# Layer 0 of a four-layer graph network in another order: P first, bias rows and polynomial between the first products

## The chip, the cores and the metric

The kernel runs on one core of a Trainium2 chip. Five queues work side by side on it: TensorE (PE, matmuls and transposes), VectorE (DVE), ScalarE (ACT), GpSimd (POOL) and SyncE (SP, which issues the DMAs). Each takes its own instructions strictly in the order in which the program wrote them, and waits for semaphores. The metric is the device time of one launch in microseconds (us). Three runs of the kernel before took 1326.53, 1332.32 and 1336.32 us.

## The reference, cut to what matters

Four layers run one after another on `x` (16 batches of 512 nodes by 128 features) with one adjacency matrix `adj` (512 x 512). Only layer 0, `x = x + L0(relu(layernorm(x)))`, is touched:

```python
h = jnp.einsum('bnd,ed->bne', x, fc_in_w) + fc_in_b
alph = sigmoid(alpha_train)[:, None]
w_eff = w * clip(d, 0, 1) @ w.T
dt = 1 / 8
def euler_step(h, _):                       # 8 times
    ax = jnp.einsum('nm,bmd->bnd', adj_mx, h)
    f = alph * 0.5 * (ax - h) + h @ w_eff - h + x0
    return (h + dt * f, None)
```

The eight steps are linear in `h`, so the kernel computes them as a polynomial of degree 8 in two matrices: P (512 x 512, `dt/2 * alph * (adj - I)`) from the left and R (128 x 128, `(1 - dt) I + dt * w_eff`) from the right. The input bias gives a polynomial too, in P applied to a vector of ones and R applied to the bias row.

## The kernel before, in words

`build_front` does layer 0, and beside it prepares the later layers (masks, attention vectors, the largest eigenvalue of the graph by repeated squaring). A barrier of all engines stands between it and `build_layers`, so what `build_front` takes is added to what the layers take.

**The head** (to about 52 us) loads `adj`, the weights and four batches of `x`. VectorE makes P (`step_weights`: `P_row`), TensorE turns it (`turn_p`, into PSUM banks 4 to 7), VectorE and ScalarE copy the turned P out (`PT`; `PT_hi` is its rounded part and `PT_lo` the rest), TensorE multiplies out P squared (`p_product(PT, ...)`, four products of four matmuls), the powers of R (`r_product`), P times ones (`p_ones`), and the products with R (`fc_products`, `bias_products`). Meanwhile the first batches go through a layer norm: `statistics(b)` on VectorE, `scale_bias(b)` on GpSimd, `relu(b)` on ScalarE, and a split into two parts, `split_z(b)`, on ScalarE and then VectorE. GpSimd also forms `asym` (adj plus its transpose), which ScalarE copies into the first matrix to be squared.

**The first chunk.** The 16 batches go in four chunks of four. For each batch of a chunk TensorE turns it (`turn_x0`), applies P and P squared (`apply_p`, whose second half waits until VectorE has emptied bank 5, `keep_u2`), in chunk 0 also makes a quarter of P cubed (`p_product(P2T, ...)`), and then does one slot of the squaring work beside it (`aside`). In the second slot the square sums go through a matmul into bank 6, VectorE takes the reciprocal (`nrm`), and TensorE may not turn the next batch into the same bank before that. Behind the four batches come three levels of products with G, the table of polynomial terms (`right_products`), and with P cubed (`p3_times`).

**G and the bias** are VectorE's: `polynomial` is 9 scalings and 36 multiply-adds of 128 x 128, `bias_levels` ends in 24 multiply-adds (12 for each power of P) and `attention_vectors` is a set of small operations for layers 1 and 2. The nine bias rows lie in `gb`, in the memory of `U2T`.

The order of the work on every engine is the order in which these calls are written out in the five blocks (`@block.vector` and so on); nothing reorders it.

Of the kernel before, what the change touches and what calls it, by code (L numbers as in the profile page):

```python
# [7 lines left out]
F32 = mybir.dt.float32  # L8
# [3 lines left out]
ALU = mybir.AluOpType  # L12
# [3 lines left out]
B, N, D = 16, 512, 128  # L16
P = 128
NT = N // P
# [6 lines left out]
STEPS = 8  # L25
# [3 lines left out]
BLOCKS = 3  # L29
# [109 lines left out]
def build_front(nc, k):  # L139
# [3 lines left out]
    with ExitStack() as c:  # L143
# [16 lines left out]
        PT, = early([("PT", [P, NT, N])])  # L160
# [16 lines left out]
        S = [k.lap_hi, k.lap_lo]  # L177
        sqr = k.mask_att[:].rearrange("p t m -> p (t m)")

        gb = U2T[:].rearrange("p t n -> p (t n)")[:, 0:(STEPS + 1) * D].rearrange("p (k d) -> p k d", d=D)  # L180
        edge_i = sb("edge_i", [P, 2, E], I32)
        node_col = sb("node_col", [P, NT])
        edge_ci = sb("edge_ci", [P, 2, ET], I32)
# [174 lines left out]
        def _(act):  # L358
# [53 lines left out]
            for s in range(NT):  # L412
                act.wait_ge(sem("adj_turned"), s + 1)
                nc.scalar.copy(asym[:, s, :], bank[4 + s][:]).then_inc(sem("adjT"), 1)
            for b in range(2):
                relu(b)
                split_z(b)
            for s in range(NT):
                act.wait_ge(sem("p_turned"), s + 1)
                nc.scalar.copy(PT_hi[:, s, :], bank[4 + s][:]).then_inc(sem("PT_hi"), 1)  # L420
            act.wait_ge(sem("asym"), NT)
            nc.scalar.copy(S[0][:], asym[:]).then_inc(sem("scaled"), 1)
            for b in range(2, CB):
# [37 lines left out]
        def _(dve):  # L461
# [10 lines left out]
            def split_z(b):  # L472
                dve.wait_ge(sem("z_hi"), b + 1)
                nc.vector.tensor_tensor(zsplit[:, b % 2, 1, :], xin[b % CB][:].rearrange("p t d -> p (t d)"),
                                        zsplit[:, b % 2, 0, :].bitcast(F32), ALU.subtract).then_inc(sem("z_lo"), 1)
# [64 lines left out]
                    nc.vector.tensor_copy(W[n][:], bank[0][:, (i + 1) * P:(i + 2) * P]).then_inc(sem("wT"), 1)  # L540
                nc.vector.tensor_copy(FR[:, 0, :], bank[1][:, 0:P]).then_inc(sem("FR"), 1)

            def p_turned(s):
                dve.wait_ge(sem("p_turned"), s + 1)
                dve.wait_ge(sem("PT_hi"), s + 1)
                nc.vector.tensor_copy(PT[:, s, :], bank[4 + s][:]).then_inc(sem("PT"), 1)
                nc.vector.tensor_tensor(PT_lo[:, s, :], bank[4 + s][:], PT_hi[:, s, :].bitcast(F32), ALU.subtract
                                        ).then_inc(sem("PT_lo"), 1)

            def p_squared(s):  # L550
# [20 lines left out]
            def r_powers(q):  # L571
                lo, hi = [(2, 2), (3, 4), (5, 8)][q]
                dve.wait_ge(sem("R_product"), q + 1)
                nc.vector.tensor_copy(Rp[:, lo:hi + 1, :],
                                      bank[2][:, 0:(hi - lo + 1) * D].rearrange("p (k d) -> p k d", d=D)
                                      ).then_inc(sem("R_power"), 1)
# [7 lines left out]

            def bias_levels():

                nc.vector.tensor_copy(gb[:, 0, :], row["fcb"]).then_inc(sem("gb"), 1)
                for q in range(2):
                    dve.wait_ge(sem("bR_product"), q + 1)
                    for m in range(4):  # L590
                        i = 1 + 4 * q + m
                        nc.vector.tensor_scalar(gb[:, i, :], bank[2 + q][:, m * D:(m + 1) * D],
                                                float(comb(STEPS, i)), None, ALU.mult).then_inc(sem("gb"), 1)
                dve.wait_ge(sem("p_one"), 2)
                dve.wait_ge(sem("gb"), STEPS + 1)
                for m in range(1, BLOCKS):
                    for lev in range(BLOCKS):
                        if m > 1:
                            dve.wait_ge(sem("bias"), (lev + 1) * NT)
                        for t in range(NT):  # L600
                            before = gb[:, STEPS - BLOCKS * lev, :] if m == 1 else bias[:, lev, t, :]
                            nc.vector.scalar_tensor_tensor(bias[:, lev, t, :], gb[:, STEPS - BLOCKS * lev - m, :],
                                                           pone[:, m - 1, t:t + 1], before, ALU.mult, ALU.add
                                                           ).then_inc(sem("bias"), 1)

            def polynomial():


                dve.wait_ge(sem("FR"), 3)
                for i in range(STEPS + 1):  # L610
                    nc.vector.tensor_scalar(G[:, i, :], FR[:, i, :], float(comb(STEPS, i)), None,
                                            ALU.mult).then_inc(sem("G_sum"), 1)
                dve.wait_ge(sem("R_power"), 4)
                for m in range(STEPS):
                    dve.wait_ge(sem("G_sum"), STEPS + 1 + sum(STEPS - i for i in range(m)))
                    for i in range(m + 1, STEPS + 1):
                        nc.vector.scalar_tensor_tensor(G[:, i, :], Rp[:, m, :], DT * comb(STEPS - i + m, STEPS - i),
                                                       G[:, i, :], ALU.mult, ALU.add).then_inc(sem("G_sum"), 1)
# [45 lines left out]
            def edge_weights():  # L664

                dve.wait_ge(sem("rows"), 3 * ET)
                for e in range(ET):
# [4 lines left out]
                nc.vector.tensor_scalar(k.seg_bias[:], k.same_src[:], BIG, -BIG, ALU.mult, ALU.add  # L672
                                        ).then_inc(sem("seg"), 1)

            for b in range(2):
                statistics(b)
            step_weights()
            for b in range(2):
                split_z(b)
            weights()  # L680
            for s in range(NT):
                p_turned(s)
            nc.vector.tensor_reduce(pone[:, 0, :], P_row[:], AX, ALU.add).then_inc(sem("p_one"), 1)
            r_first()
            for b in range(2, CB):
                statistics(b)
            r_powers(0)
            r_powers(1)
            for s in range(2):
                p_squared(s)  # L690
            r_powers(2)
            for s in range(2, NT):
                p_squared(s)
            dve.wait_ge(sem("p_ones"), 1)
            nc.vector.tensor_copy(pone[:, 1, :], bank[3][:, 0:NT]).then_inc(sem("p_one"), 1)
            products_with_r()
            attention_vectors()
            bias_levels()
            polynomial()
            slot = 0  # L700
            for ch in range(NCH):
                for j in range(CB):
                    b = ch * CB + j
                    if j < CB - 2:
                        split_z(b + 2)
                    keep_u2(b)
                    if ch == 0:
                        p_cubed(j)
                    aside(slot)
                    slot += 1  # L710
                for lev in range(BLOCKS):
                    for t in range(NT):
                        if lev < BLOCKS - 1:
                            z_sum(ch, lev, t)
                            if lev == 0 and ch < NCH - 1:
                                statistics((ch + 1) * CB + t)
                            if lev == 0:
                                z_low(ch, lev, t)
                        else:
                            final(ch, t)  # L720
                            if t < 2 and ch < NCH - 1:
                                split_z((ch + 1) * CB + t)
                        aside(slot)
                        slot += 1
                        if ch == NCH - 1 and lev == 0 and t == 0:
                            top_eigenvalue()
                        elif ch == NCH - 1 and lev == 0 and t == 1:
                            for s in range(NT):
                                laplacian(s)
                            dve.wait_ge(sem("lap"), NT)  # L730
                            for s in range(NT):
                                diagonal = lap[:, s, cols(s)]
                                nc.vector.tensor_tensor(diagonal, diagonal, k.ident[:], ALU.subtract
                                                        ).then_inc(sem("lap"), 1)
                        elif ch == NCH - 1 and lev == 0 and t == 2:
                            edge_numbers()
                    if lev == 1:
                        for t in range(NT):
                            z_low(ch, lev, t)
# [15 lines left out]
        def _(pe):  # L755
# [162 lines left out]
            turn_adj("adj_turned", None)  # L918
            turn_weights()
            turn_p()  # L920
            w_eff()
            pe.wait_ge(sem("PT"), NT)
            pe.wait_ge(sem("PT_lo"), NT)
            p_product(PT, 0, 4, "p_square")
            r_product(0)
            p_product(PT, 1, 5, "p_square")
            r_product(1)
            p_product(PT, 2, 6, "p_square")
            r_product(2)
            p_product(PT, 3, 7, "p_square")  # L930
            p_ones()
            fc_products()
            bias_products()
            pe.wait_ge(sem("P2T_lo"), NT)
            slot = 0
            for ch in range(NCH):
                for j in range(CB):
# [1100 lines left out]
```

## Time and profile before

| | us |
|---|---|
| median of three runs | 1332.32 (1326.53 to 1336.32) |
| the profiled execution | 1326.59 |
| its span in the trace | 1324.8 |
| TensorE busy | 1176.4 (89%) |
| VectorE busy | 784.3 (59%) |
| ScalarE busy | 762.5 (58%) |
| GpSimd busy | 473.9 (36%) |

The span is the time from the first to the last instruction in the trace; the execution's own time is 1.8 us more. TensorE is busy for nine tenths. Its clock has two levels, 1.2 and 2.4 GHz; the column PEclk gives the granted clock as a share of the higher one (0.50 is 1.2 GHz), and its mean over the execution is 0.957.

### The profile page before, as it was taken

To read this page: it belongs to the slowest core of one execution; us is meant where nothing else is said; L and a number is where in the kernel's file an instruction comes from. 1 tells how busy PE (TensorE), PEld (TensorE's weight loads), DVE (VectorE), ACT (ScalarE), POOL (GpSimd) and SP (SyncE) were. 2 spreads that over 40 slices of the span, in tenths; PEclk is the share of its full clock that TensorE was granted. 3 is DMA by queue.
4 is the path that set the end of the run, shared out by engine and by line. 5 is a ranking of instruction groups with operands and counts; after the bars stand their busy time and mean duration, and the time that the engine had idled before them with its cause. 6 is when DMAs were issued, how large, how long until landed. Compare 5 with 4: busy or idle time off the path is not lost. (4 is left out here: it accounts for less than half of the span.)

```text
span 1324.8 us, 24887 instructions
## 1 busy us (share of the span) xinstructions
PE 1176.4 (89%) x7613; PEld 920.3 (69%) x7613; DVE 784.3 (59%) x2837; ACT 762.5 (58%) x1612; POOL 473.9 (36%) x578
## 2 busy tenths in 40 slices
PE   4979999999999547899999999999999999999763
PEld 3658878888889435677776777777777677766542
DVE  6623213213332234677888888888888888866652
ACT  4213324234211023487888788788888878885770
POOL 4203003003125022335346445644644654552423
PEclk7989999999999768999999999999999999998996
DMA  4001020020200100223323423432432342343311
GB/s 117 16 17 33 24 65 8 25 72 1 64 9 9 32 8 17 66 68 99 90 71 97 112 64 87 111 89 62 111 95 62 97 111 65 86 104 86 96 51 31
DMA packets 123748, 83.68 MB, mean 63 GB/s; under 512 B 13216, under 2 KB 106784, under 8 KB 123680
## 3 DMA queue, kind: packets, MB, share of 16 engines
q1 hardware_dynamic: 123680, 82.82, 23.8%
q8 instruction: 37, 0.61, 0.2%
q14 instruction: 31, 0.25, 0.1%
HBM read 28.25 MB, written 20.97 MB: 37 GB/s over the span
## 5 line engine op out<-in xcount | busy, mean ns | idle before, releaser
L1726 DVE CUSTOM_DVE_ANT_0 att_Ts<-bank,mask_att 128x512 f32<-128x512 f32 x256 | 173.5, 685 | 71.7 <-PE bank L1811 70.2
L1521 ACT ACTIVATE att_Es<-att_Ts,att_small 128x512 f32<-128x512 f32 x256 | 184.6, 721 | 39.0 <-DVE att_small L1726 38.1
L1951 PE MATMUL bank<-ident,att_Es 128*128 128x128 f32 x1024 | 157.2, 276 | 23.3 <-ACT att_PTs L1529 22.7
L1529 ACT COPY att_PTs<-bank 128x512 f32<-128x512 f32 x256 | 147.5, 576 | 32.1 <-PE bank L1951 31.3
L1951 PEld LDWEIGHTS bank<-ident,att_Es 128*128 128x128 f32 x1024 | 118.5, 142 | 67.3 <-issue 29.8
L1811 PE MATMUL bank<-K_parts,Q_parts 128*128 128x512 f32 x256 | 125.6, 500 | 9.0 <-DMA K_parts<-k_lo 8.8
L290 POOL TENSOR_SCALAR l_rs<-l_mv 128x4 f32<-128x4 f32 x16 | 6.9, 431 | 251.3 <-DVE l_mv L470 251.1
L1456 POOL TENSOR_SCALAR gat_Vs<-gat_Ts,gat_small 128x512 f32<-128x512 f32 x64 | 62.4, 989 | 54.4 <-DVE gat_small L1603 54.4
L484 DVE TENSOR_TENSOR P_row<-bank,l_bias 128x512 f32<-128x512 f32 x32 | 22.1, 691 | 99.2 <-PE bank L855 77.8
L845 PE MATMUL bank<-G,x0T 128*128 128x128 f32 x384 | 75.0, 277 | 1.2 <-DVE U2T L479 1.0
L845 PE MATMUL bank<-G,U1T 128*128 128x128 f32 x384 | 74.4, 275 | 0.0
L845 PE MATMUL bank<-G,U2T 128*128 128x128 f32 x384 | 74.3, 275 | 0.0
L1327 POOL TENSOR_SCALAR n_rs<-n_mv 128x4 f32<-128x4 f32 x48 | 11.2, 234 | 160.5 <-DVE n_mv L1322 160.3
L1811 PEld LDWEIGHTS bank<-K_parts,Q_parts 128*128 128x128 f32 x256 | 47.6, 191 | 29.0 <-issue 26.7
L845 PEld LDWEIGHTS bank<-G,x0T 128*128 128x128 f32 x384 | 60.9, 191 | 5.4 <-issue 2.4
L1850 PE MATMUL bank<-gat_whs,gat_ETs 128*128 128x128 f32 x512 | 63.8, 280 | 0.7 <-ACT gat_ETs L1500 0.7
L1850 PEld LDWEIGHTS bank<-gat_whs,gat_ETs 128*128 128x128 f32 x512 | 62.0, 196 | 1.7 <-ACT gat_ETs L1500 1.1
L845 PEld LDWEIGHTS bank<-G,U2T 128*128 128x128 f32 x384 | 58.4, 192 | 0.0
L845 PEld LDWEIGHTS bank<-G,U1T 128*128 128x128 f32 x384 | 58.3, 192 | 0.0
L1972 PE MATMUL bank<-att_PTs,v_in 128*32 128x512 f32 x512 | 57.9, 592 | 0.0
L1494 ACT ACTIVATE gat_Ts<-gat_Vs,gat_small 128x512 f32<-128x512 f32 x64 | 45.9, 719 | 17.4 <-DVE gat_Vs L1608 17.2
L388 ACT CAST Z_hi<-P_row 128x512 fp32r<-128x512 f32 x32 | 18.6, 617 | 62.9 <-DVE P_row L484 44.3
(307 smaller groups left out, 3101.2 us busy)
## 6 DMA issues: line engine op xcount, KB each, us to landing
Q_parts<-q_hi SPq DMA_DIRECT2D x128, 64.0 KB, 2.0
Q_parts<-q_lo SPq DMA_DIRECT2D x128, 64.0 KB, 2.0
K_parts<-k_hi SPq DMA_DIRECT2D x128, 64.0 KB, 2.0
K_parts<-k_lo SPq DMA_DIRECT2D x128, 64.0 KB, 2.0
l_x<-in_x SPq DMA_DIRECT2D x16, 256.0 KB, 2.9
P2T<-in_x SPq DMA_DIRECT2D x16, 256.0 KB, 4.2
x_after_l<-P2T SPq DMA_DIRECT2D x16, 256.0 KB, 2.3
gat_xin<-x_after_l SPq DMA_DIRECT2D x16, 256.0 KB, 2.9
```

Source lines behind the costliest of these rows:

```text
L388: nc.scalar.copy(Z_hi[:, t, :], zs[:, t, :]).then_inc(sem("l0_Zhi"), 1)
L484: nc.vector.tensor_tensor(by_batch(zs[:, t, :]), by_batch(bank[t][:]), bias[:, BLOCKS - 1 - lev, t:t + 1, :].broadcast_to([P, CB, D]), ALU.add
L845: mm = nc.tensor.matmul(bank[t][:, b * D:(b + 1) * D], UT[i][:, b, cols(t)], G[:, STEPS - k0 - i, :], start=(b == 0 and i == 0), stop=(lev ...
L1456: nc.gpsimd.tensor_scalar(gat_V[:, t, :], gat_T[:, t, :], 0.2, gat_small[:, 5, t:t + 1], ALU.mult, ALU.add).then_inc(sem("gat_low"), 1)
L1494: nc.scalar.activation(gat_E[:, t, :], gat_V[:, t, :], ACT.Exp, bias=gat_small[:, 4, t:t + 1], accum_out=gat_small[:, 6, t:t + 1]).then_in ...
L1521: nc.scalar.activation(att_E[:, j % RING_E, :], att_T[:, j % RING_T, :], ACT.Exp, scale=-1.0, bias=att_small[:, 0, j:j + 1], accum_out=att ...
L1529: nc.scalar.copy(att_PT[:, i // NT, :, cols(i % NT)], c2[:].rearrange("p (s q) -> p s q", q=P)).then_inc(sem("att_pt"), 1)
L1726: nc.vector.tensor_tensor_reduce(att_T[:, j % RING_T, :], [c0, c1][j % 2][:], k.mask_att[:, j % NT, :], -QK_SCALE, HUGE, ALU.add, ALU.min, ...
L1811: return nc.tensor.matmul(dst, left, right, start=True, stop=True)
L1850: mm = nc.tensor.matmul(a0[:, cols(t)], gat_ET[:, s, cols(t)], WhA[:, s, :], start=(s == 0), stop=(s == NT - 1))
L1951: mm = nc.tensor.transpose(c2[:, cols(s)], att_E[:, i % RING_E, cols(s)], k.ident[:])
L1972: mm = nc.tensor.matmul(b0[r, :], vD[:, s, r], att_PT[:, h, s, :], start=(s == 0), stop=(s == NT - 1))
```

## The change

Nothing is computed that was not computed before, save that `PT_hi` and `PT_lo` are made from the copy `PT` in SBUF and not from PSUM. What moves:

- **VectorE, head**: `step_weights` comes first, then the four copies of `PT` as soon as each is turned, then the weights, the four `PT_lo`, `r_first`, and only then `statistics(0)` and `(1)`. `split_z(0)` and `(1)` stand behind `r_powers(2)`.
- **ScalarE, head**: the four `PT_hi` stand ahead of `relu(0)`.
- **TensorE, head**: the first product of P squared waits for `PT` alone and stands ahead of `w_eff`; the R products stand one product of P later. The wait for `PT_lo` is at the start of chunk 0.
- **VectorE, first chunk**: `bias_levels` keeps the making of the nine rows, which now lie in `src_rows` and `seg_bias`. The rest is cut up and set behind `p_cubed(j)` of batch j: the 9 scalings and the first 12 multiply-adds of the bias (j = 0), 15 terms of the polynomial (j = 1), the other 21 (j = 2), the last 12 of the bias and the attention vectors (j = 3).

```diff
-        gb = U2T[:].rearrange("p t n -> p (t n)")[:, 0:(STEPS + 1) * D].rearrange("p (k d) -> p k d", d=D)
+        gb = [k.src_rows[:].rearrange("p e n -> p (e n)")[:, i * D:(i + 1) * D] for i in range(STEPS)]
+        gb.append(k.seg_bias[:, 0, 0:D])
@@ ScalarE
+            for s in range(NT):
+                act.wait_ge(sem("PT"), s + 1)
+                nc.scalar.copy(PT_hi[:, s, :], PT[:, s, :]).then_inc(sem("PT_hi"), 1)
             for b in range(2):
                 relu(b)
                 split_z(b)
-            for s in range(NT):
-                act.wait_ge(sem("p_turned"), s + 1)
-                nc.scalar.copy(PT_hi[:, s, :], bank[4 + s][:]).then_inc(sem("PT_hi"), 1)
@@ VectorE
-            def p_turned(s):
+            def keep_p(s):
                 dve.wait_ge(sem("p_turned"), s + 1)
+                nc.vector.tensor_copy(PT[:, s, :], bank[4 + s][:]).then_inc(sem("PT"), 1)
+
+            def p_low(s):
                 dve.wait_ge(sem("PT_hi"), s + 1)
-                nc.vector.tensor_copy(PT[:, s, :], bank[4 + s][:]).then_inc(sem("PT"), 1)
-                nc.vector.tensor_tensor(PT_lo[:, s, :], bank[4 + s][:], PT_hi[:, s, :].bitcast(F32), ALU.subtract
+                dve.wait_ge(sem("PT"), s + 1)
+                nc.vector.tensor_tensor(PT_lo[:, s, :], PT[:, s, :], PT_hi[:, s, :].bitcast(F32), ALU.subtract
                                         ).then_inc(sem("PT_lo"), 1)
...
             def bias_levels():
 
-                nc.vector.tensor_copy(gb[:, 0, :], row["fcb"]).then_inc(sem("gb"), 1)
+                dve.wait_ge(sem("late_loaded"), 16 * len(late_loads))
+                nc.vector.tensor_copy(gb[0], row["fcb"]).then_inc(sem("gb"), 1)
...
-            def polynomial():
-
+            def polynomial_first():
 
                 dve.wait_ge(sem("FR"), 3)
                 for i in range(STEPS + 1):
                     nc.vector.tensor_scalar(G[:, i, :], FR[:, i, :], float(comb(STEPS, i)), None,
                                             ALU.mult).then_inc(sem("G_sum"), 1)
+
+            def polynomial(terms):
+
                 dve.wait_ge(sem("R_power"), 4)
-                for m in range(STEPS):
+                for m in terms:
...
+            step_weights()
+            for s in range(NT):
+                keep_p(s)
+            weights()
+            for s in range(NT):
+                p_low(s)
+            r_first()
             for b in range(2):
                 statistics(b)
-            step_weights()
-            for b in range(2):
-                split_z(b)
-            weights()
-            for s in range(NT):
-                p_turned(s)
             nc.vector.tensor_reduce(pone[:, 0, :], P_row[:], AX, ALU.add).then_inc(sem("p_one"), 1)
-            r_first()
+            r_powers(0)
             for b in range(2, CB):
                 statistics(b)
-            r_powers(0)
             r_powers(1)
             for s in range(2):
                 p_squared(s)
             r_powers(2)
+            for b in range(2):
+                split_z(b)
             for s in range(2, NT):
                 p_squared(s)
...
             products_with_r()
-            attention_vectors()
             bias_levels()
-            polynomial()
...
                     keep_u2(b)
                     if ch == 0:
                         p_cubed(j)
+                        if j == 0:
+                            polynomial_first()
+                            bias_of(1)
+                        elif j == 1:
+                            polynomial(range(2))
+                        elif j == 2:
+                            polynomial(range(2, STEPS))
+                        else:
+                            bias_of(2)
+                            attention_vectors()
                     aside(slot)
@@ TensorE
             turn_p()
+            pe.wait_ge(sem("PT"), NT)
+            p_product(PT, 0, 4, "p_square")
             w_eff()
-            pe.wait_ge(sem("PT"), NT)
-            pe.wait_ge(sem("PT_lo"), NT)
-            p_product(PT, 0, 4, "p_square")
+            p_product(PT, 1, 5, "p_square")
             r_product(0)
-            p_product(PT, 1, 5, "p_square")
+            p_product(PT, 2, 6, "p_square")
             r_product(1)
-            p_product(PT, 2, 6, "p_square")
+            p_product(PT, 3, 7, "p_square")
             r_product(2)
-            p_product(PT, 3, 7, "p_square")
             p_ones()
             fc_products()
             bias_products()
             pe.wait_ge(sem("P2T_lo"), NT)
+            pe.wait_ge(sem("PT_lo"), NT)
```

VectorE at the start of the head, before (`BN_STATS` and `BN_AGGR` are `statistics`, `sg` the sigmoid's steps, `bank` is PSUM):

```order
L467 BN_STATS l_stats<-l_x 128x6 x4
L470 BN_AGGR l_mv<-l_stats 128x2 x4
...
L522 TENSOR_SCALAR P_row<-adj,sg 128x512 x4
L527 SCALAR_TENSOR_TENSOR P_row<-ident,sg,P_row 128x128 x4
L474 TENSOR_TENSOR z_split<-l_x,z_split 128x512 x2
L533 TENSOR_SCALAR dclip<-dcol 128x1
...
L546 COPY PT<-bank 128x512
L547 TENSOR_TENSOR PT_lo<-bank,PT_hi 128x512
```

And now:

```order
L523 TENSOR_SCALAR P_row<-adj,sg 128x512 x4
L528 SCALAR_TENSOR_TENSOR P_row<-ident,sg,P_row 128x128 x4
L546 COPY PT<-bank 128x512 x4
L534 TENSOR_SCALAR dclip<-dcol 128x1
...
L551 TENSOR_TENSOR PT_lo<-PT,PT_hi 128x512 x4
L568 TENSOR_SCALAR Rp<-bank 128x128
L570 COPY Rp<-ident 128x128
L572 SCALAR_TENSOR_TENSOR Rp<-ident,Rp 128x128
L468 BN_STATS l_stats<-l_x 128x6 x4
L471 BN_AGGR l_mv<-l_stats 128x2 x4
```

The copies of the turned P stand right behind the making of P, and the first `statistics` behind the first power of R, which waits for TensorE's `w_eff`.

VectorE from the bias rows into the first chunk, before (`U2T` first holds the bias rows, then `keep_u2`'s copy; `l_bias` is the bias of the levels, `nrm` the reciprocal that TensorE waits for):

```order
L592 TENSOR_SCALAR U2T<-bank 128x128 x8
L602 SCALAR_TENSOR_TENSOR l_bias<-U2T,pone 128x128 x12
L602 SCALAR_TENSOR_TENSOR l_bias<-U2T,pone,l_bias 128x128 x12
L611 TENSOR_SCALAR G<-FR 128x128 x9
L617 SCALAR_TENSOR_TENSOR G<-Rp,G 128x128 x36
L474 TENSOR_TENSOR z_split<-l_x,z_split 128x512
L479 COPY U2T<-bank 128x512
L558 TENSOR_TENSOR P3T_lo<-bank,P3T_hi 128x512
L474 TENSOR_TENSOR z_split<-l_x,z_split 128x512
L479 COPY U2T<-bank 128x512
L558 TENSOR_TENSOR P3T_lo<-bank,P3T_hi 128x512
L503 RECIPROCAL nrm<-bank 128x1
```

And now:

```order
L480 COPY U2T<-bank 128x512
L562 TENSOR_TENSOR P3T_lo<-bank,P3T_hi 128x512
L616 TENSOR_SCALAR G<-FR 128x128 x9
L608 SCALAR_TENSOR_TENSOR l_bias<-src_rows,pone,seg_bias 128x128 x4
L608 SCALAR_TENSOR_TENSOR l_bias<-src_rows,pone 128x128 x8
L475 TENSOR_TENSOR z_split<-l_x,z_split 128x512
L480 COPY U2T<-bank 128x512
L562 TENSOR_TENSOR P3T_lo<-bank,P3T_hi 128x512
L625 SCALAR_TENSOR_TENSOR G<-Rp,G 128x128 x15
L504 RECIPROCAL nrm<-bank 128x1
L480 COPY U2T<-bank 128x512
L562 TENSOR_TENSOR P3T_lo<-bank,P3T_hi 128x512
```

The copy that empties bank 5 now stands ahead of the polynomial, and the reciprocal stands behind 15 of its terms.

## Rows read from the trace of the kernel before

**Rows 1.** Window: length, busy us of PE, PEld, DVE, ACT, POOL; PEclk, DMA, GB/s.
```profile
104.00:160.00 56.00, 55.55 (x379) 50.55 (x378) 18.19 (x55) 21.59 (x39) 12.78 (x20) 1.00 0.10 29
```

**Rows 2.** Timeline of TensorE: start, duration, what, and idle time before it.
```profile
7.06 3.43 PE L761 MATMUL bank<-ident,adj 128*128 128x128 f32 x16 [7.06 <-DMA adj<-in_adj]
...
10.76 0.27 PE L768 MATMUL bank<-ident,raw_fcw 128*128 128x128 f32 x1
15.08 3.67 PE L775 MATMUL bank<-ident,P_row 128*128 128x128 f32 x16 [4.05 <-DVE P_row L527]
...
25.92 5.98 PE L781 MATMUL bank<-PT,P_row 128*128 128x512 f32 x8 [4.02 <-DVE PT_lo L547]
...
43.55 3.63 PE L816 MATMUL bank<-pone,PT 128*128 128x1 f32 x32
47.04 3.19 PE L801 MATMUL bank<-Rp,raw_fcw 128*128 128x512 f32 x4
...
52.26 0.60 PE L824 MATMUL bank<-ident,l_x 128*128 128x128 f32 x4
```

**Rows 3.** Timeline of TensorE in chunk 0.
```profile
61.34 1.49 PE L862 MATMUL bank<-lap_hi 128*128 128x512 f32 x4
...
72.24 0.80 PE L836 MATMUL bank<-P2T_hi,z_split 128*128 128x512 f32 x1 [6.18 <-DVE U2T L479]
...
83.02 0.66 PE L824 MATMUL bank<-ident,l_x 128*128 128x128 f32 x4 [1.36 <-DVE nrm L503]
...
103.90 0.38 PE L845 MATMUL bank<-G,x0T 128*128 128x128 f32 x2
```

**Rows 4.** Timeline of VectorE in the head.
```profile
9.14 0.87 DVE L467 BATCH_NORM_STATS2 l_stats<-l_x 128x6 f32<-128x128 f32 x4 [9.14 <-DMA l_x<-in_x]
...
12.18 1.68 DVE L522 TENSOR_SCALAR P_row<-adj,sg 128x512 f32<-128x512 f32 x4
...
15.09 1.77 DVE L474 TENSOR_TENSOR z_split<-l_x,z_split 128x512 fp32r<-128x512 f32 x1
...
20.91 0.68 DVE L546 COPY PT<-bank 128x512 f32<-128x512 f32 x1
```

**Rows 5.** Timeline of VectorE: attention vectors, bias rows, bias, polynomial.
```profile
50.87 0.28 DVE L624 CUSTOM_DVE_ANT_0 junk<-w_W1g,a_rows 128x128 f32<-128x128 f32 x1
...
53.09 0.23 DVE L587 COPY U2T<-rowv 128x128 f32<-128x128 f32 x1
...
58.18 3.23 DVE L602 SCALAR_TENSOR_TENSOR l_bias<-U2T,pone,l_bias 128x128 f32<-128x128 f32 x12
...
62.75 8.24 DVE L617 SCALAR_TENSOR_TENSOR G<-Rp,G 128x128 f32<-128x128 f32 x36
```

**Rows 6.** Timeline of GpSimd.
```profile
15.04 5.83 POOL L317 TENSOR_TENSOR asym<-adj,asym 128x512 f32<-128x512 f32 x4
29.91 0.23 POOL L290 TENSOR_SCALAR l_rs<-l_mv 128x4 f32<-128x4 f32 x1 [9.03 <-DVE l_mv L470]
...
33.95 7.11 POOL L322 TENSOR_SCALAR mask_gat<-adj 128x2048 bf16<-128x2048 f32 x1
...
121.10 5.03 POOL L329 TENSOR_TENSOR P2T<-P2T,l_bias 128x512 f32<-128x512 f32 x4
```

**Rows 7.** Timeline of ScalarE.
```profile
33.90 1.65 ACT L363 ACTIVATE l_x<-l_x,l_rs 128x128 f32<-128x128 f32 x4 [0.37 <-POOL l_rs L298]
35.45 1.04 ACT L427 CAST P2T_hi<-bank 128x512 fp32r<-128x512 f32 x2
```

**Rows 8.** Windows where the granted clock (PEclk) is low or changes; columns as in Rows 1.
```profile
15.00:19.00 4.00, 3.67 (x16) 3.27 (x16) 3.35 (x5) 3.90 (x10) 4.00 (x4) 0.50 0.56 78
...
30.00:31.00 1.00, 1.00 (x3) 0.44 (x2) 0.95 (x7) 0.00 (x0) 0.84 (x3) 0.71 0.00 0
...
68.00:69.00 1.00, 0.00 (x0) 0.00 (x0) 0.96 (x6) 0.00 (x0) 0.00 (x0) 0.56 0.00 0
...
78.00:80.00 2.00, 2.00 (x5) 0.76 (x4) 1.29 (x2) 0.44 (x1) 0.00 (x0) 0.91 0.00 0
```

More of the change, by code:

```diff
@@ L591, in bias_levels, with bias_of @@
                         i = 1 + 4 * q + m
-                        nc.vector.tensor_scalar(gb[:, i, :], bank[2 + q][:, m * D:(m + 1) * D],
+                        nc.vector.tensor_scalar(gb[i], bank[2 + q][:, m * D:(m + 1) * D],
                                                 float(comb(STEPS, i)), None, ALU.mult).then_inc(sem("gb"), 1)
+            def bias_of(m):
                 dve.wait_ge(sem("p_one"), 2)
                 dve.wait_ge(sem("gb"), STEPS + 1)
[L596 to L604, printed above, removed]
-            def polynomial():
+                for lev in range(BLOCKS):
+                    if m > 1:
+                        dve.wait_ge(sem("bias"), (lev + 1) * NT)
+                    for t in range(NT):
+                        before = gb[STEPS - BLOCKS * lev] if m == 1 else bias[:, lev, t, :]
+                        nc.vector.scalar_tensor_tensor(bias[:, lev, t, :], gb[STEPS - BLOCKS * lev - m],
+                                                       pone[:, m - 1, t:t + 1], before, ALU.mult, ALU.add
+                                                       ).then_inc(sem("bias"), 1)
+            def polynomial_first():
                 dve.wait_ge(sem("FR"), 3)
```

## The prediction

> **What bounds the kernel now.** I read the windows by stage first. Behind its first chunk layer 0 is TensorE's: 55.55 of 56 us busy, clock 1.00 [rows 1]. So whatever brings TensorE to that stage earlier is kept: the later chunks do not make it up or wait for anything the change moves, and a barrier stands before the layers. Only the first 104 us matter. Next comes TensorE's timeline, where the reader is to see the gaps. In the head it idles 4.05 us for VectorE's P and 4.02 us for VectorE's last `PT_lo` [rows 2]. From 43.55 it is busy to the first batch at 52.26. In chunk 0 it idles 6.18 us until VectorE has emptied bank 5, and 1.36 us for the reciprocal [rows 3]. Last come VectorE's timeline, which shows what it did meanwhile (layer norm ahead of P; attention vectors, bias and polynomial ahead of the bank) [rows 4, 5], and GpSimd's and ScalarE's, for who waits for the layer norm that is now put back [rows 6, 7].
>
> **Step 1: P earlier.** `adj` has landed at 7.06, when TensorE starts on it; VectorE begins P at 12.18 only, behind two statistics, and TensorE turns it 2.9 us later, at 15.08 [rows 2, 4]. Now P is begun at 7.1 and ready at 10.0. TensorE has the weights to turn until 11.0 [rows 2], so the turn starts at 10.9. It took 3.67 us at clock 0.50 [rows 2, 8]. The first 16 transposes took 0.21 each, but the five behind them 0.11 (10.49 to 11.03), so the clock was up there in fact, and without the 4 us gap I expect most of the turn at that pace: 1.8 us is the lower end. VectorE copies each bank in 0.68 [rows 4]. The last copy ends between 14.1 (four copies in a row) and 15.3 (slow turn). I take 14.3.
>
> **Step 2: the products.** From the first product's end (31.90) to `p_ones` (43.55) there are 11.65 us for 6144 columns of P and 896 of R: 3.4 us for a product of 2048, 0.2 for `w_eff` [rows 2]. So: first product to 17.8 (it took 5.98 at a low clock before, rising at 30.6 [rows 2, 8]), `w_eff` to 18.0, the rest to 29.7, `p_ones` (3.5) to 33.2. Before, that was 47.04: TensorE is **13.8 us ahead** here.
>
> **Step 3: the new wait in the head.** `fc_products` needs the last powers of R, and VectorE takes them behind `p_squared(0)` and `(1)`, which wait for ScalarE's `P2T_hi`, which stand behind `relu(3)`, which waits for GpSimd, which works through `asym` first, which stands behind `scale_bias(0)` and `(1)`, which need the statistics that now come last. In numbers: `w_eff` 18.0; three small operations at 0.23 (8.24 over 36 [rows 5]) to 18.8; two statistics at 1.2 each (with four small operations they fill the 3.04 us between 9.14 and 12.18 [rows 4]), the first ready at 20.0. GpSimd: two `scale_bias` take 3.95 (29.91 to ScalarE's start without further wait, 33.86 [rows 6, 7]) to 24.0; `asym` 5.0 (5.83 before, beside VectorE's own traffic; a set of the same shape took 5.03 [rows 6]) to 29.0; two more `scale_bias` to 33.0. ScalarE: `relu` 1.65 and a cast 0.5 [rows 7] to 35.2. VectorE: four operations at 0.68 and the copy of the powers to 38.6. TensorE therefore idles 5.4 us, and its lead shrinks to 8.4.
>
> **Step 4: the rest of the head.** `fc_products` has 1024 columns: 1.7 us at the full clock. The clock was low for part of it before (fc and bias together took 52.26 - 47.04 = 5.2 for 3.4 [rows 2]) and now an idle stretch follows, so I take twice 1.7: to 42.0. `bias_products` waits for the second `p_one`, behind two `split_z` and two `p_squared`. Beside `asym` a `split_z` took 1.77 against the 0.68 of an undisturbed operation of its size [rows 4, 6], 1.1 more for the first of the two: VectorE is through at 38.6 + 1.1 + 6 x 0.68 + 0.2 = 44.0. The Trainium skill, page "SBUF — State Buffer" (section "Terms", shared port pair), says such an operation is locked out for the whole of a GpSimd instruction; `mask_gat` is a single one of 7.11 us, running here from 33.0 to 40.1, so by the rule the first `split_z` waits 1.5, and the sum would be 0.4 us worse. The 1.77 row agrees with it. Two bias matmuls at either level, 1.7 to 3.4, I take 2.6: chunk 0 starts at 46.6, **5.7 us ahead**.
>
> **Step 5: chunk 0.** A batch step takes (103.90 - 83.02) / 2 = 10.44 us at clock 1.00 [rows 3]. Batch 0 ends at 57.0. Bank 5 is emptied during it, since only the copy and a subtraction stand ahead of the bias terms: the 6.18 us gap goes, and so do the 6.1 us at low clock behind it (72.24 to 78.36 [rows 3, 8]), worth 3.05. Batch 1's cube ends at 66.1 (10.44 less the square, 1.3 [rows 3]). **The new wait**: the reciprocal stands behind ScalarE's cast (0.6), the subtraction (0.68) and 15 terms at 0.23, 3.4 us: ready at 71.0, where TensorE was ready at 66.3. It idles 4.7 us where it idled 1.36. The clock fell 2 us into such a gap (68:69 shows 0.56, TensorE having stopped at 72.24 - 6.18 = 66.06) [rows 3, 8] and came back 4.7 us after the restart at 25.92 and 6.1 after that at 72.24 [rows 2, 3, 8]: 5.4 us low, 2.7 lost. Batches 2 and 3 then end at 71.0 + 20.9 + 2.7 = 94.6, 9.3 ahead. The other 21 terms (4.8 us) lie beside batch 3 and cost nothing: G is wanted at 94.6, ready before 90.
>
> **Step 6: the first level.** Behind the last cube (T) VectorE has the subtraction at T + 1.3, then 12 bias terms (3.23) and the attention vectors (53.09 - 50.87 = 2.2) [rows 5]: free at T + 6.7. TensorE's first level tile (1536 columns, 2.5 us) is ready at T + 3.8. The sum is 2.9 late, and behind it on ScalarE stand a cast and the scaling that the second squaring needs, at T + 8.7; TensorE gets there at T + 7.5. Cost 1.2 us; ends 0 and 2.9. The lateness ends within the level: a tile with its square is 3.7 us on TensorE, and 2.6 on VectorE (sum 0.68, statistics 1.2, subtraction 0.68). The extra wait for `late_loaded` costs nothing: the statement it gates runs at 45, and the attention vectors passed the same wait at 50.87 without idling.
>
> **Sum.** 5.7 (head) + 6.2 + 3.05 (gap and clock gone) - 3.3 (4.7 for 1.36) - 2.7 (clock) - 1.2 (level) = 7.8 us (rounding aside): 1326.59 becomes **1318.8** in an execution like the profiled one. That execution lies at the low end of the times shown (their median is 1332.32; all four average 1330.4), so the median to expect is 1330.4 - 7.8 = **1322.6**.
>
> **Rivals.**
> - *Low clock through the first product* (20%). The turn and the first product run at 0.50, as before [rows 2, 8]: last copy 15.3, product 5.98 to 21.3, 3.5 us later than in step 2, and the whole chain of step 3 hangs on its end. Gain 4.3: 1326 for the median. For it: 15:19 shows 0.50 all through the 16 transposes. Against: the five transposes at 0.11. The Trainium skill, page "TensorE: Matmul & The Clock Gate" (section "Part 4: PE-mode transpose"), says that transposes do not count as busy time for the clock in the way that matmuls do; by that rule this rival is the outcome, and only the 0.11 row speaks against it.
> - *The clock holds in both new gaps* (15%). Then 2.7 is not lost in batch 2, and the bias products take 1.7 instead of 2.6: gain 11.4, median 1319. Against: the fall 2 us into the gap at 66.
> - *The new order is late where it matters* (5%), the case that ends slower. The reciprocal's wait restarts TensorE at the low clock, and the clock stays low for the rest of the chunk, because the gaps (5.4, 2, 4.7 us) come before it has risen for good. From 46.6 TensorE has 41.8 us of full-clock work; each of these at the low level costs one more. It decides at 8 + 3 us of such work beyond what is counted; if all of batches 0 to 3 ran low, 39 us more than forecast: 1361. Against: every restart in this trace got its clock back within 6.1 us.
> - *Nothing to speak of is left* (5%). If the chain of step 3 is 5.7 us longer than priced (each of its hand-overs between engines late, `asym` at its dearest), chunk 0 starts at 52.3 as before, and the gain is the 2.1 us of steps 5 and 6: median 1328.
> - My forecast, its waits as priced: 55%.
>
> **Range and chances.** Unknown costs: step 1, 1 us; step 3, 0.8 for `asym`; step 4, 0.9; step 5, 1; step 6, 1.7. With the neighbours on both sides the gain lies between 3 and 12; the runs of one kernel spread by ±5 around their middle, of which a median of a few keeps about 3. So 1314 to 1331. Beyond 1%, 13.3 us, is about what a measurement here can tell from no change. The forecast stays inside it, and only a gain at the upper end together with a favourable draw passes it: faster 0.20, same 0.75, slower 0.05.
>
> **What would show it.** In the changed trace: the first product of P squared starting near 14.3 and lasting 3.6 (not 5.98); `fc_products` idle for about 5 us, released by VectorE's copy of the powers, with `P2T_hi` on ScalarE starting near 35 behind `relu`; no gap before batch 1's second half; about 4.7 us idle before batch 2's turning, released by `nrm`; and the first G product near 95 instead of 103.90. The prediction is wrong if `fc_products` does not wait (gain 10 and more), or if a gap stands behind the first chunk that is not there now.

## The result, and the profile after

The changed kernel took 1316.5 us (median of 4 runs, 1314.62 to 1318.01) against 1331.05 (4 runs, 1326.53 to 1336.32): ratio 0.9894, interval 0.9861 to 0.9926. Timed again, 12 runs against 29, the ratio was 0.9924, interval 0.9898 to 0.9951: 10 us or 0.8%. The forecast of 1322.6 (1314 to 1331) holds, on the modest side: the measured gain is larger.

The profiled execution took 1317.77 us, span 1316.0 (before: 1326.59 and 1324.8). TensorE after, timeline of the head; columns as in [rows 2]:

```profile
6.91 3.68 PE L779 MATMUL bank<-ident,adj 128*128 128x128 f32 x16 [6.91 <-DMA adj<-in_adj]
10.38 0.42 PE L785 MATMUL bank<-ident,raw_w 128*128 128x128 f32 x1
...
11.17 0.27 PE L786 MATMUL bank<-ident,raw_fcw 128*128 128x128 f32 x1
11.28 1.91 PE L793 MATMUL bank<-ident,P_row 128*128 128x128 f32 x16
14.45 3.70 PE L799 MATMUL bank<-PT,P_row 128*128 128x512 f32 x8 [1.27 <-DVE PT L546]
...
30.03 3.63 PE L834 MATMUL bank<-pone,PT 128*128 128x1 f32 x32
38.69 3.52 PE L819 MATMUL bank<-Rp,raw_fcw 128*128 128x512 f32 x4 [5.03 <-DVE Rp L578]
42.44 1.96 PE L826 MATMUL bank<-Rp,fcb_b 128*128 128x512 f32 x4 [0.24 <-DVE pone L705]
44.23 0.60 PE L842 MATMUL bank<-ident,l_x 128*128 128x128 f32 x4
```

The turn of P is at 11.28 and takes 1.91 us (15.08 and 3.67 in [rows 2]), the first product 3.70 in place of 5.98, `p_ones` is 13.5 us earlier, and then TensorE waits 5.03 us where it did not wait before. TensorE after, timeline of chunk 0 and its first level, against [rows 3]:

```profile
54.64 0.60 PE L842 MATMUL bank<-ident,l_x 128*128 128x128 f32 x4
...
68.90 0.96 PE L842 MATMUL bank<-ident,l_x 128*128 128x128 f32 x4 [4.51 <-DVE nrm L504]
...
80.94 0.60 PE L842 MATMUL bank<-ident,l_x 128*128 128x128 f32 x4
...
91.36 0.38 PE L863 MATMUL bank<-G,x0T 128*128 128x128 f32 x2
...
99.21 1.21 PE L880 MATMUL bank<-lap_lo 128*128 128x512 f32 x4 [1.40 <-ACT lap_lo L399]
```

The 6.18 us gap is gone. In place of 1.36 us TensorE waits 4.51 for `nrm`, batch 2 takes 12.04 us (80.94 - 68.90) where batch 3 takes 10.42, and the first G product is 12.5 us earlier than at 103.90. In the first level there is a new wait of 1.40. The layers begin (first L1801 before, L1819 after, both `bank<-ident,gat_z`) at 461.76 before and at 450.98 now, 10.8 us sooner:

```profile
461.76 1.12 PE L1801 MATMUL bank<-ident,gat_z 128*128 128x128 f32 x4 [11.66 <-DVE gat_z L1354]
```
```profile
450.98 1.11 PE L1819 MATMUL bank<-ident,gat_z 128*128 128x128 f32 x4 [11.70 <-DVE gat_z L1372]
```

Of these 10.8 us the span shows 8.8, because the layers, whose code is the same, took 863.0 us in the one execution and 865.0 in the other. Over the 14 traces of this document that same code took 860.6 to 870.7 us, so a gain of a few us is read here from the start of the layers and from the ratio of several executions, never from one total.

### The profile page after: what moved, and what is told of

It is laid out like the page before. It is cut to its first block and busy times, and to the rows that moved or that the text cites. A ratio compares the mean times of both kernels' runs of the same rounds, so it can differ in the third digit from the quotient of the medians.

```text
span 1316.0 us, 24888 instructions
## 1 busy us (share of the span) xinstructions
PE 1175.7 (89%) x7613; PEld 922.1 (70%) x7613; DVE 781.3 (59%) x2837; ACT 763.0 (58%) x1612; POOL 473.5 (36%) x578
```

## The experiments

Of e5, e6 and e8 there is one execution each, so only their traces speak, and they have no ratio.

**e1, the change again.** No edit.

> The changed kernel once more, to size the gain. Theory A (the gain is all in layer 0): the traces have the layers start at 461.76 before and 450.98 after, so the ratio is 10.8 / 1331 below one, 0.9919, and the start of the layers lies again near 451. Theory B (the layers gain too, since the medians lie 14.5 us apart): ratio 0.989 or less, and the stretch from the start of the layers to the end is some 4 us shorter than before's.

Ratio 0.9924 (0.9898 to 0.9951); layers start at 450.84, and take 1315.8 - 450.84 = 865.0 us again. Theory A holds: the gain is in layer 0, 10.1 us by the ratio and 10.8 in the traces, and the 14.5 us between the first medians of four runs each are at least in part their scatter.

**e2, the head alone.** From the change:

```diff
             products_with_r()
+            attention_vectors()
             bias_levels()
+            bias_of(1)
+            bias_of(2)
+            polynomial_first()
+            polynomial(range(STEPS))
...
-                        if j == 0:
-                            polynomial_first()
-                            bias_of(1)
...
```

> The new head, but attention vectors, bias and polynomial again in one piece ahead of chunk 0. If the two parts add up: chunk 0 starts near 44.2 (8.0 ahead of before), the 6.2 us gap ahead of batch 1's second half and the low clock behind it are back, the first G product comes near 96, and the gain is 8.0 us (ratio 0.994). Rival: the pieces of the head and the chunk are worth nothing alone, since VectorE's block ends at the same time as before: then the gap grows by the 8 us and the ratio is 1.000.

Ratio 0.9972 (0.9950 to 0.9994), 3.7 us. Chunk 0 starts at 44.40, and the gap of before is back at 6.71 us (6.18), not 8 us longer: VectorE's block shifts with the head. The rival falls. TensorE of e2, timeline:

```profile
64.92 0.80 PE L849 MATMUL bank<-P2T_hi,z_split 128*128 128x512 f32 x1 [6.71 <-DVE U2T L480]
```

The first G product is at 95.87, 8.0 ahead as expected. The gain expected of the whole, 8.0 us (0.994), did not come: 0.994 lies outside the interval. The layers start at 455.70, 6.1 ahead; the table behind e12 shows where the rest went.

**e3, the chunk alone.** The head's order on VectorE, ScalarE and TensorE is that of before, the rest that of the change.

> The old head, with bias terms, polynomial and attention vectors spread over chunk 0 as in the change. If the two parts add up: chunk 0 starts at 52.3, no gap in batch 1, 4.5 us idle ahead of batch 2 and a low clock behind it, first G product near 99.4 (4.5 ahead), 1.7 us given back in the first level: gain 2.8 us (ratio 0.998). Rival: the spreading is the main part (6.2 of gap and 3 of clock) and the waits it adds are small: gain 7 or more (0.995).

Ratio 0.9984 (0.9954 to 1.0013). First G product at 100.59: 3.3 ahead, where 4.5 were expected. Batch 2 took 12.92 us there (77.27 to 90.19) and 12.04 in the change, for the same work behind the same 4.51 us wait: the length of the low clock differs. Together 8.0 + 3.3 = 11.3, against 12.5 for the change. The head is the larger part. By the totals that sum cannot be confirmed: 3.7 and 2.1 us by the ratios, and the layers of e3 start at 462.01, no earlier than before (461.76).

**e4, reciprocal ahead of the terms.**

```diff
                         p_cubed(j)
+                    aside(slot)
+                    slot += 1
+                    if ch == 0:
                         if j == 0:
...
-                    aside(slot)
-                    slot += 1
```

> The changed kernel with each batch's slot of squaring work (the reciprocal in batch 1) ahead of the terms of the polynomial on VectorE. If the 4.5 us gap ahead of batch 2 is the wait for the reciprocal behind 15 terms: the gap is 1.5 us as in before, the clock holds, batch 2 takes 10.5 and not 12.0 us, and the kernel gains 4.6 us on the change (ratio to before 0.988 if the change is at 0.992). Rival (TensorE would have waited there for something else, such as the cast of P cubed or the copy of bank 5): less than 1 us gained and another releaser.

TensorE of e4, timeline:

```profile
65.78 0.66 PE L843 MATMUL bank<-ident,l_x 128*128 128x128 f32 x4 [1.36 <-DVE nrm L504]
...
76.25 0.60 PE L843 MATMUL bank<-ident,l_x 128*128 128x128 f32 x4
...
86.66 0.38 PE L864 MATMUL bank<-G,x0T 128*128 128x128 f32 x2
```

The wait is 1.36, batch 2 takes 10.47, the first G product comes 4.7 us earlier than in the change. The 3.15 us of wait above 1.36 belonged to the 15 terms and to nothing else. Ratio to before 0.9902 (0.9870 to 0.9934), where 0.988 was expected: 2.9 us better than the change by the ratios, and 2.8 at the start of the layers, against 4.7 at the first G product. The intervals of the two overlap, so the totals alone do not tell e4 from the change.

**e5, matmuls in the gap.**

```diff
+                    if b == 2:
+                        for i in range(5):
+                            nc.tensor.matmul(bank[2][:], P_row[:, 0, 0:P], PT_hi[:, 0, :].bitcast(F32), start=True, stop=True)
                     need(pe, sem("nrm"), normed[0])
```

> The changed kernel with five matmuls of 128x512 (4.3 us at the full clock, their result unused) on TensorE in front of its wait for the reciprocal. The wait's end is VectorE's, near 68.9. If batch 2 is slow (12.0 us in place of 10.5) because the clock fell in the gap: it takes 10.5 now, the granted clock stays at 1.00 from 68 to 80, and the first G product comes 1.6 us earlier, near 89.8. Rival (batch 2 is slow because VectorE's 21 terms or ScalarE hold it): still 12.0 us.

Windows of e5 and of the change over that stretch; columns as in [rows 1]:

```profile
68.00:70.00 2.00, 1.88 (x8) 0.78 (x7) 1.55 (x8) 0.41 (x1) 0.00 (x0) 1.00 0.00 0
70.00:72.00 2.00, 2.00 (x12) 1.64 (x11) 0.00 (x0) 0.86 (x2) 0.00 (x0) 1.00 0.19 55
```
```profile
68.00:80.00 12.00, 11.10 (x37) 7.79 (x37) 1.54 (x6) 1.86 (x3) 0.00 (x0) 0.86 0.08 23
```

The clock stays at 1.00 and batch 2 takes 10.47 us (69.61 to 80.08), 1.57 less than in the change. From the gap's start to the first G product it is 25.7 us (64.81 to 90.49) against 27.2 (64.12 to 91.36). The head of this run was 0.7 us late, so the expected 89.8 came out as 90.49. What the low clock costs behind the wait is 1.6 us. The execution as a whole took 1324.63 us: its layers, whose code is the same, took 870.7 us, the longest of all.

**e6, asym first on GpSimd.** The loop over `asym` stands ahead of `scale_bias(0)`.

> The changed kernel with GpSimd's asym ahead of scale_bias(0) and (1). If the wait of fc_products hangs on GpSimd's queue: relu(3) ends near 32, P2T_hi is cast from there, fc_products starts near 35.8 (38.7 in the change), its wait shrinks from 5.0 to about 2, and chunk 0 starts some 2.9 us earlier, at 41.4. Rival (it hangs on VectorE, which reaches the copy of the powers no sooner): fc_products stays within 0.5 us of 38.7.

`fc_products` starts at 37.24 with 1.80 us of wait: 1.4 us sooner, not 2.9. Its timelines (VectorE, GpSimd) show why:

```profile
8.77 4.18 DVE L526 SCALAR_TENSOR_TENSOR P_row<-ident,sg,P_row 128x128 f32<-128x128 f32 x4
```
```profile
8.90 5.17 POOL L316 TENSOR_TENSOR asym<-adj,asym 128x512 f32<-128x512 f32 x4 [6.59 <-ACT asym L413]
```

Four multiply-adds on P that take 1.14 us in the change take 4.18 beside `asym`; the turn starts 1.7 us late, at 13.01. Chunk 0 starts at 43.49, not at 41.4. The wait does hang on GpSimd's queue, but `asym` there costs VectorE.

**e7, statistics early on VectorE.** `statistics(0)` and `(1)` behind the four copies of `PT`.

> The changed kernel with statistics(0) and (1) on VectorE right behind the four copies of PT, where TensorE does the first product. The chain through GpSimd and ScalarE then starts 3.5 us sooner; w_eff waits 0.2 us for the weights. Expected: no wait or under 0.5 us ahead of fc_products (start 33.8), chunk 0 near 39.5, gain 4.7 us on the change, ratio to before 0.989. Rival (w_eff and r_first, pushed back 2.4 us on VectorE, hold the R products and so TensorE): first R product late, gain under 2 us.

`fc_products` at 36.68 with 1.98 us of wait, not 33.8; chunk 0 at 43.43, only 0.8 us sooner. Ratio 0.9896 (0.9870 to 0.9923), within the scatter of the change's own; in its trace the layers start at 453.03, 2.0 us later than in the change. GpSimd of e7, timeline:

```profile
18.91 3.22 POOL L296 TENSOR_TENSOR l_rs<-l_rs,neg_half 128x4 f32<-128x4 f32 x1
```

This small operation takes 1.04 us elsewhere. It lies beside VectorE's four `PT_lo` subtractions (18.73 to 21.22) and took 2.2 us more. The bound moved, and low clock took most of the rest: `bias_products` lasted 3.16 us against 1.96. The expectation missed by 3.9 us.

**e8, attention vectors behind batch 2's terms**, with a wait for the last bias terms ahead of the level.

> The changed kernel with the attention vectors behind batch 2's terms, 2.2 us less in front of the first level. If the 1.4 us wait in the first level is VectorE's lateness there: the first sum starts near 95.0 (97.2 in the change), the wait for the scaled matrix ahead of the second squaring is gone or under 0.3 us, and the start of the third level is 1.4 us earlier. Rival (the squaring is paced by ScalarE's own queue): the 1.4 us stay.

The first sum starts at 94.95 (97.22 in the change) and the wait of 1.40 is gone. It was VectorE's lateness. The layers nevertheless start at 451.30 (450.98): the low clock in the later chunks took it back.

**e9, asym last.** On GpSimd `asym` behind `scale_bias(3)`, on ScalarE its copy behind `P2T_hi`.

> The changed kernel with asym behind all four scale_bias on GpSimd and its copy behind P2T_hi on ScalarE, so that nothing on either queue stands between the statistics and P2T_hi that it doesn't need. If fc_products waits for that chain: relu(3) ends near 30.8, fc_products starts near 34.5 with under 1 us of wait (5.0 in the change), and no operation of VectorE or GpSimd is stretched, as P_row was in asym first and l_rs in statistics early. Chunk 0 then starts near 41, not the full 4.2 us sooner, since more of fc_products and bias_products falls into the low clock. Gain on the change 3 us, ratio to before 0.990. Rival (the low clock takes all of it, as in statistics early): chunk 0 within 1 us of 44.2.

The first half came true, `fc_products` at 34.51 with 0.79 of wait. Then `bias_products` waits 4.78 us, chunk 0 starts at 45.71, later than in the change, and the ratio is 0.9971 (0.9945 to 0.9996). VectorE and GpSimd of e9, timelines:

```profile
34.37 5.46 DVE L473 TENSOR_TENSOR z_split<-l_x,z_split 128x512 fp32r<-128x512 f32 x2
```
```profile
34.17 7.11 POOL L321 TENSOR_SCALAR mask_gat<-adj 128x2048 bf16<-128x2048 f32 x1
```

and the same two in the change:

```profile
38.55 1.28 DVE L475 TENSOR_TENSOR z_split<-l_x,z_split 128x512 fp32r<-128x512 f32 x2
```
```profile
33.45 7.11 POOL L323 TENSOR_SCALAR mask_gat<-adj 128x2048 bf16<-128x2048 f32 x1
```

Begun 0.2 us behind `mask_gat` the two operations take 5.46 us; begun 5.1 us behind it they take 1.28.

**e10, the three moves together** (e4, e8, e9).

> Reciprocal ahead of the terms, asym last and attention vectors behind batch 2's terms, together on the changed kernel. If the three waits are separate: first G product near 83.5 (91.4 in the change), no wait above 1.4 us in chunk 0 and its first level, layers start near 442, gain 9 us on the change, ratio to before 0.985 to 0.986. Rival (the gains overlap, because batches that run closer together leave VectorE behind with its terms): a new wait for U2T or G, gain under 6.

First G product at 88.39 where 83.5 was expected, layers at 446.13 (442), ratio 0.9901 (0.9866 to 0.9935) where 0.985 to 0.986 was: the expectation missed. What e4 and e8 gave stayed (waits of 1.36 and none), and `bias_products` again waited, 5.05 us.

**e11, and mask_gat held back.**

```diff
                 if ch == 0:
+                    pool.wait_ge(sem("z_lo"), 2)
                     nc.gpsimd.tensor_scalar(k.mask_gat[:], adj[:], 0.0, -BIG, ALU.is_equal, ALU.mult
```

> The kernel of e10 with one wait more on GpSimd: mask_gat does not start before both split_z are through. If the 5.46 us that two split_z took in e9 and e10 (1.28 in the change) came from mask_gat, begun 0.2 us ahead of them: they take 1.3 again, bias_products waits under 0.5 us in place of 5.05, chunk 0 starts near 41.3 (45.98 in e10), first G product near 83.7 (88.39), ratio to before 0.986 to 0.987. Rival (the two split_z wait for something else, such as the end of ScalarE's copy of asym at 36.1): bias_products still near 42.5.

VectorE and TensorE of e11, timelines:

```profile
34.19 1.28 DVE L474 TENSOR_TENSOR z_split<-l_x,z_split 128x512 fp32r<-128x512 f32 x2
```
```profile
38.09 1.98 PE L827 MATMUL bank<-Rp,fcb_b 128*128 128x512 f32 x4 [0.34 <-DVE pone L704]
39.91 0.60 PE L843 MATMUL bank<-ident,l_x 128*128 128x128 f32 x4
...
82.33 0.38 PE L864 MATMUL bank<-G,x0T 128*128 128x128 f32 x2
```

One wait on GpSimd brings chunk 0 from 45.98 to 39.91, and the first G product to 82.33. It is the fastest version: 1305.32 us against 1327.9, ratio 0.9850 (0.9814 to 0.9887), clear of the change's own interval (0.9898 to 0.9951). ScalarE's copy of `asym` stood where it did in e10, so it was not the cause.

**e12, only e4 and e8.**

> Only the two moves on VectorE in chunk 0 that did what they should in e4 and e8: the reciprocal ahead of the terms and the attention vectors behind batch 2's; the head is the change's. If they add up: chunk 0 starts at 44.2, first G product near 86.7, no wait of 1.4 us in the first level, layers start near 446.5 (450.98 in the change), gain 6 us on the change where the clock falls out alike, ratio to before 0.988. Rival: one of the two waits comes back in another place, and the gain is that of e4 alone (4.6 us, 0.989).

First G product at 86.84, no wait in the first level, layers at 444.73; ratio 0.9900 (0.9868 to 0.9932). In the trace they add up (446.5 was expected for the layers); by the ratio e12 is no better than e4 alone (0.9902), and the expected 0.988 did not come.

**The runs side by side.** How far each run's first G product and its layers start ahead of before's (103.90 and 461.76), in us. The third column is an estimate of what the low clock cost between the two, worked out from the PEclk of the windows of 4 us between 104 and 420: each counts 4 x (1 - PEclk). For before it is 1.7.

| run | first G product | low clock cost | layers | ratio |
|---|---|---|---|---|
| e1, the change | 12.7 | 1.7 | 10.9 | 0.9924 |
| e2, head alone | 8.0 | 3.4 | 6.1 | 0.9972 |
| e3, chunk alone | 3.3 | 3.4 | -0.3 | 0.9984 |
| e4 | 17.2 | 3.4 | 13.6 | 0.9902 |
| e5 | 13.4 | 5.1 | 9.7 | |
| e6 | 12.6 | 3.4 | 9.0 | |
| e7 | 12.4 | 3.4 | 8.7 | 0.9896 |
| e8 | 12.7 | 3.4 | 10.5 | |
| e9 | 10.0 | 3.4 | 6.7 | 0.9971 |
| e10 | 15.5 | 1.7 | 15.6 | 0.9901 |
| e11 | 21.6 | 0 | 22.7 | 0.9850 |
| e12 | 17.1 | 1.7 | 17.0 | 0.9900 |

From the first G product to the layers, less this cost and less 1.4 where the first level waits, each run takes 356.1 to 356.7 us, before and the first trace of the change too; only e5 takes 355.0. So the low clock in the later chunks, and the 1.4 where the first level waits, explain why a lead at the first G product is not always kept.

## Why the prediction was right, step by step

| | before | forecast | after |
|---|---|---|---|
| first product of P starts | 25.92 | 14.3 | 14.45 |
| `p_ones` ends, next in line | 47.04 | 33.2 | 33.6 |
| `fc_products` starts | 47.04 | 38.6 | 38.69 |
| chunk 0 starts | 52.26 | 46.6 | 44.23 |
| wait for the reciprocal | 1.36 | 4.7 | 4.51 |
| lost to the clock in batch 2 | | 2.7 | 1.6 |
| first G product | 103.90 | 94.6 | 91.36 |
| wait in the first level | | 1.2 | 1.40 |
| gain at the start of the layers | | 7.8 | 10.8 |

**Steps 1 to 3 held.** P was begun at 6.95, the transposes ran at 0.12 each, and the chain over `w_eff`, statistics, GpSimd, `relu` and `P2T_hi` ended within 0.1 us of the forecast. That closeness is partly luck: GpSimd and ScalarE were 0.4 us later than counted (VectorE's first copy of P squared at 35.55, not 35.2), and VectorE's five operations behind it 0.4 shorter, since they start 0.60 apart and not 0.68. e6 and e9 show that this chain is what `fc_products` waits for: with `asym` out of it the wait is 0.79. The price of 5.0 for `asym` was right (4.94).

**Step 4 was too dear by 2.4 us.** The two `split_z` were priced 1.1 us up for GpSimd's `mask_gat` and took no more than alone (1.28); VectorE's operations follow each other in 0.60, where I counted their recorded 0.68, six times; and the clock came back at 41.8, 3.1 us after the restart, so that the bias products ran at full clock, 1.8 and not 2.6. e9 to e11 show that the conflict with `mask_gat` is real but ends before `mask_gat` does in the record, and that the order of the change happened to miss it.

**Step 5**: the wait was right, and e4 and e5 tell its two parts apart: 3.15 us of time (4.51 for 1.36) and 1.6 of clock. The forecast had the clock fall 2 us into the gap and stay low for 5.4 us of batch 2. It did neither. Windows of the change:

```profile
66.00:68.00 2.00, 0.00 (x0) 0.00 (x0) 1.97 (x11) 0.00 (x0) 0.00 (x0) 1.00 0.00 0
68.00:69.00 1.00, 0.10 (x1) 0.10 (x2) 0.85 (x5) 0.12 (x1) 0.00 (x0) 1.00 0.00 0
69.00:70.00 1.00, 1.00 (x5) 1.00 (x6) 0.00 (x0) 0.67 (x2) 0.00 (x0) 0.56 0.00 0
72.00:73.00 1.00, 1.00 (x4) 0.81 (x4) 0.00 (x0) 0.00 (x0) 0.00 (x0) 0.74 0.11 31
```

PEclk is 1.00 all through the idle stretch and falls near 69.1, 0.2 us behind the restart at 68.90; it is back near 72.5, 3.6 us after the restart, where before it took 4.7 and 6.1. So TensorE worked 3.4 us at the low level, not 5.4, and lost 1.6, not 2.7. That is 1.1 us of the difference. My column of times has a slip beside the sum: it puts 9.3 us from batch 1's start to its last matmul where both traces have 9.75, which is why it came to a lead of 9.3 at the first G product and the terms of the sum to 8.95. **Step 6** was right in mechanism and size (e8). The sum was 3.0 us short in all: 2.4 of step 4 and 1.1 of the clock, less 0.2 for the longer wait in the first level. These make 3.3; the 0.3 too much I cannot assign.

**The rivals.** Low clock through the first product: refuted, the product took 3.70. The Trainium skill's page "TensorE: Matmul & The Clock Gate" (section "Part 4: PE-mode transpose") would have had it so; here TensorE had done nothing but transposes since 6.91 when their spacing fell from 0.21 to 0.11 us near 11.0, so the trace disagrees. This rests on their pace: the column PEclk reads 1.00 there from 7 us on, also where the spacing was 0.21. The clock holding in the gaps: it was low behind both, and e5, which filled the second, kept it. Nothing left and a slower kernel: the medians of the change are 1316.5 and 1316.87 us, against 1328 and 1361, and the layers start 10.8 and 10.9 us sooner.

The remaining distance to the first measured ratio (14.5 us against 10.8 in the traces) I take for the draw of the runs, since the ratio of e1, from more of them, gives 10.1. So the forecast median of 1322.6 was off by 6.1 us, about half of it the 3.0 of the sum.

## What to carry to other kernels

Where an engine takes its work strictly in order, ask of every long block which of its operations somebody waits for, and put these ahead of the rest: the head, with P and four copies ahead of a layer norm, gave 8.0 us at the first G product (e2), and one reciprocal ahead of 15 terms 4.7 (e4). At the start of the layers 6.1 and 2.8 were left. A move that shortens one queue can bring two engines' operations side by side that were apart; look in the new trace for operations whose duration grew, before blaming the dependence. And give a long instruction that nobody waits for (here a mask recorded with 7.11 us) a wait for the urgent ones of its neighbour: e11 against e10 gained 6.1 us that way at the first G product.

## What the runs showed of the hardware that I had not expected

- VectorE and GpSimd hold each other up, in both directions: four multiply-adds of VectorE took 4.18 for 1.14 us beside `asym`, two subtractions 5.46 for 1.28 beside `mask_gat`, and a 4-column GpSimd operation 3.22 for 1.04 beside VectorE's subtractions. The Trainium skill, page "SBUF — State Buffer" (section "Terms", shared port pair), says that the loser is blocked for the other's full instruction. The direction agrees. The extent does not for `mask_gat`: in e9 VectorE was free again at 34.37 + 5.46 - 1.28 = 38.55, 4.4 us after the start of an instruction recorded with 7.11, and in the change, 5.1 us behind its start, nothing was held. Whether the block ends ahead of the instruction or the record has the instruction too long, no trace here tells. The row that the prediction called in agreement falls short of the rule too: that `split_z` began 0.05 us behind an `asym` instruction of 1.46 (5.83 over 4), so the rule would make it 2.1, and it took 1.77.
- Not every VectorE operation is held. In e11 `mask_gat` starts at 35.56. The operations that read PSUM beside it keep their 0.68, and the first copy from SBUF to SBUF, 0.21 us in the change, takes 3.71 in the record; the next one starts at 40.08, 4.5 us behind the start of `mask_gat`. VectorE of e11, timeline:

```profile
37.19 0.68 DVE L556 TENSOR_TENSOR P2T_lo<-bank,P2T_hi 128x512 fp32r<-128x512 f32 x1
...
39.05 3.71 DVE L591 COPY src_rows<-rowv 128x128 f32<-128x128 f32 x1
```

- Where the low clock falls in the later chunks differs between kernels whose order of work is the same there; the two executions of the change agree (376:384 at 0.79 in both). Before, the window 176:184 of layer 0 shows PEclk 0.79 and the stretch at 376 none; after, it is the window 376:384:

```profile
176.00:184.00 8.00, 6.78 (x25) 5.57 (x26) 1.17 (x3) 1.86 (x3) 0.00 (x0) 0.79 0.13 33
```
```profile
376.00:384.00 8.00, 8.00 (x61) 8.00 (x60) 3.84 (x10) 0.62 (x1) 0.00 (x0) 0.79 0.00 0
```

  The same wait for `nrm` stands in both, with the low clock behind it before and without it after (TensorE, timelines of before and of the change):

```profile
177.22 1.04 PE L824 MATMUL bank<-ident,l_x 128*128 128x128 f32 x4 [2.05 <-DVE nrm L503]
```
```profile
166.35 0.66 PE L842 MATMUL bank<-ident,l_x 128*128 128x128 f32 x4 [2.05 <-DVE nrm L504]
```

  That wait of 2.05 us cost 1.7 us of clock or nothing, and a low clock in and behind 32 matmuls of 128x1 (as in `p_ones`), not before, cost 1.7 us in the change and 3.4 in e2, which is where the window 376:384 above lies. What decides between them no run here shows. So one trace locates a gain of this size only up to the point where it arises, and with 6 to 12 executions of a kernel the ratio still has 0.3% to 0.4% either way.
